# A selective-scan megakernel: the silus of x and z in four half-sized instructions a segment, and the last dt block's pieces at other steps

## What is computed

```python
def _mamba(x, in_w, conv_w, conv_b, xproj_w, dt_w, dt_b, A_log, D, out_w):
    xz = einsum('bld,ed->ble', x, in_w); xi, z = split(xz, 2)
    xi = silu(_dw_conv(xi, conv_w, conv_b))           # 512 channels, 4 taps
    dtr, Bm, Cm = split(einsum('bld,ed->ble', xi, xproj_w))
    dt = softplus(einsum('blr,dr->bld', dtr, dt_w) + dt_b)
    for t:  h = exp(dt_t * A) * h + (dt_t * x_t) * B_t ;  y_t = sum_s h * C_t     # 16 states per channel
    y = (y + xi * D) * silu(z)
    return einsum('bld,ed->ble', y, out_w)
fwd = _mamba(h, fm...) ; bwd = _mamba(flip(h), bm...)
```

## Time and profile before

| | us |
|---|---|
| median of 3 runs | 1098.32 |
| lowest, highest | 1097.88, 1099.91 |
| profiled execution, its own time | 1099.44 |
| its span | 1097.7 |

### The profile page before, as it was taken

How to read it: one execution, slowest core, us unless ns; L and a number is a source line. 1 busy time by engine, 2 the same in 40 slices (tenths; PEclk the granted TensorE clock), 3 DMA queues, 4 the chain that set the end, 5 groups by cost and what they waited for, 6 DMA issues and landing times. The chain is left out here.

```text
span 1097.7 us, 13218 instructions
## 1 busy us (share of the span) xinstructions
PE 959.0 (87%) x3836; PEld 600.4 (55%) x3836; DVE 873.2 (80%) x1136; ACT 560.8 (51%) x1204; POOL 703.3 (64%) x505
## 2 busy tenths in 40 slices
PE   5898867999999999995969977989889987787798
PEld 2566646888888888883424422433444342332487
DVE  3788677777778778776579899988998999999853
ACT  2687632333333333322667766766577467564141
POOL 3377623555555555541289799989998899999000
PEclk9899988999999999997979999989999899999999
DMA  3000025442442442313065555654545455664001
GB/s 102 1 2 0 1 110 152 123 134 82 119 134 88 112 134 94 108 39 91 13 161 155 163 152 145 147 161 142 153 140 157 125 146 154 153 154 115 0 1 39
DMA packets 60033, 115.32 MB, mean 105 GB/s; under 512 B 10400, under 2 KB 15776, under 8 KB 59856
## 3 DMA queue, kind: packets, MB, share of 16 engines
q1 hardware_dynamic: 58848, 112.87, 36.7%
q10 hardware_dynamic: 1136, 1.90, 0.5%
HBM read 113.24 MB, written 1.51 MB: 105 GB/s over the span
## 5 line engine op out<-in xcount | busy, mean ns | idle before, releaser
L1649 POOL TENSOR_TENSOR uB<-u,rows_B 128x512 f32<-128x512 f32 x256 | 320.4, 1282 | 17.1 <-DVE da L1799 13.7
L870 POOL TENSOR_TENSOR lutw<-lutw,lt 128x865 f32<-128x865 f32 x80 | 184.9, 2312 | 164.9 <-DVE lt L836 159.1
L1818 PE MATMUL ya<-hV,ident 128*128 128x512 f32 x336 | 189.6, 651 | 62.6 <-DVE hV L1741 61.9
L1799 DVE TENSOR_TENSOR_SCAN da<-da,uB 128x512 f32<-128x512 f32 x168 | 201.0, 1220 | 17.2 <-ACT da L1728 12.3
L1818 PEld LDWEIGHTS ya<-hV,ident 128*128 128x128 f32 x336 | 61.3, 201 | 158.9 <-DVE hV L1741 123.4
L1658 POOL TENSOR_TENSOR hP<-hS,rows_C 128x512 f32<-128x512 f32 x88 | 112.7, 1281 | 21.8 <-issue 8.5
L1727 ACT ACTIVATE da<-zero 128x2 f32<-128x2 f32 x256 | 43.0, 168 | 152.0 <-DVE hV L1741 151.7
L1796 DVE TENSOR_TENSOR_SCAN hS<-da,uB 128x512 f32<-128x512 f32 x88 | 106.7, 1212 | 16.0 <-ACT da L1727 7.5
L1741 DVE TENSOR_TENSOR hV<-da,rows_C 128x512 f32<-128x512 f32 x168 | 112.6, 671 | 0.0
L744 ACT ACTIVATE ah<-ups 128x1024 fp32r<-128x1024 f32 x40 | 41.2, 1029 | 130.0 <-DVE ups L832 130.0
L829 DVE TENSOR_TENSOR si<-gps,cwb 128x1024 f32<-128x1024 f32 x40 | 49.0, 1225 | 57.1 <-ACT gps L741 53.4
(11 more groups left out here) (341 smaller groups left out, 2034.8 us busy)
## 6 DMA issues: line engine op xcount, KB each, us to landing
rows_B<-bc_rows SPq DMA_DIRECT2D x128, 256.0 KB, 3.6
rows_C<-bc_rows SPq DMA_DIRECT2D x128, 256.0 KB, 4.3
wr<-in_moe_w SPq DMA_DIRECT2D x40, 384.0 KB, 4.8
cwb<-cw_rows SPq DMA_DIRECT2D x16, 512.0 KB, 4.0
cwb<-cw_rows SPq DMA_DIRECT2D x16, 384.0 KB, 5.0
cwb<-cw_rows SPq DMA_DIRECT2D x16, 256.0 KB, 4.1
lut_f<-in_lut_idx SPq DMA_DIRECT2D x1, 2160.0 KB, 10.3
cwb<-cw_rows SPq DMA_DIRECT2D x16, 128.0 KB, 4.4
```

The source lines that it names most:

```text
L870: e.tensor_tensor(part, part, lt[:, q, :], ALU.add).then_inc(s_la, 1)
L1649: e.tensor_tensor(uB[:, n % UBUF, :], u[:, seg % 2, d, :], RB[:, q, :], ALU.mult).then_inc(s_ub, 1)
L1799: e.tensor_tensor_scan(a[:, way], a[:, way], uB[:, n % UBUF, way], 0.0, ALU.mult, ALU.add).then_inc(s_sc, 1)
L1818: return e.matmul(ya[n % 2][:, :], g.ident[:, :], at, start=False, stop=False, skip_group_check=True).then_inc(done, 1)
```

## The change

`silu_x` and `silu_z` each take a half h and work on two blocks (128x1024 instead of 128x2048), with their own table load behind. For the next segment, x's halves stand at steps 23 and 31 (before: all at 31); z's halves stand at step 62 of the segment before and at step 4 (before: all at 4). The matmul of dt block 3 moves from step 15 to step 12, its `parts` from 22 to 18, `exp` from 24 to 20, `log` from 25 to 22, its softplus on DVE from 25 to 22, and `keep_dt` from 29 to 27. In the last segment the first four of them move from 15, 21, 22, 23 to 12, 18, 20, 22.

```diff
@@ project_tensor, rows_tensor
-                              (11, x_tensor(e, k, 2)), (13, conv_tensor(e, k, 1)), (15, None), (16, x_tensor(e, k, 3)),
+                              (11, x_tensor(e, k, 2)), (12, None), (13, conv_tensor(e, k, 1)), (16, x_tensor(e, k, 3)),
-            e.wait_ge(s_xi, DB + k)
+            e.wait_ge(s_xi, DB + 2 * k)
@@ scalar
-        def silu_x(e, k):
-            e.wait_ge(s_cv, DB * k)
-            e.activation(xi[:, k % 2, :, :], xi[:, k % 2, :, :], ACT.Silu).then_inc(s_xi, 1)
-        def silu_z(e, k):
-            e.wait_ge(s_zc, DB * (k + 1))
-            e.activation(sz[:, k % 2, :, :], sz[:, k % 2, :, :], ACT.Silu).then_inc(s_sz, 1)
+        def silu_x(e, k, h):
+            two = slice(2 * h, 2 * h + 2)
+            e.wait_ge(s_cv, DB * (k - 1) + 2 * h + 2)
+            e.activation(xi[:, k % 2, two, :], xi[:, k % 2, two, :], ACT.Silu).then_inc(s_xi, 1)
+            e.preload_act_table_set("natural_log_exp_and_others")
+        def silu_z(e, k, h):
+            two = slice(2 * h, 2 * h + 2)
+            e.wait_ge(s_zc, DB * k + 2 * h + 2)
+            e.activation(sz[:, k % 2, two, :], sz[:, k % 2, two, :], ACT.Silu).then_inc(s_sz, 1)
+            e.preload_act_table_set("natural_log_exp_and_others")
@@ project_scalar
             yield 18
             copy_x(e, k, 2)
+            parts(e, k - 1, 3)
+            yield 20
+            exp(e, k - 1, 3)
             yield 21
             copy_conv(e, k, 1)
             newest_tap(e, k, 2)
             yield 22
-            parts(e, k - 1, 3)
+            log(e, k - 1, 3)
             yield 23
             copy_x(e, k, 3)
-            yield 24
-            exp(e, k - 1, 3)
-            yield 25
-            log(e, k - 1, 3)
+            silu_x(e, k, 0)
             yield 26
             copy_conv(e, k, 2)
             newest_tap(e, k, 3)
-            yield 29
+            yield 27
             keep_dt(e, k - 1, 3)
             yield 30
             copy_conv(e, k, 3)
             yield 31
-            silu_input(e, k)
+            silu_x(e, k, 1)
@@ first_scalar, middle_scalar (the end of each)
+            yield 62
+            silu_z(e, k, 0)
@@ begin_scalar
             yield 4
-            silu_z(e, seg)
-            e.preload_act_table_set("natural_log_exp_and_others")
+            silu_z(e, seg, 1)
@@ side_vector
-            yield 25 if k < NSEG else 23
+            yield 22
             softplus(e, seg, 3)
```

More of the change, by code:

```diff
@@ L1251, in side_tensor @@
             if k == NSEG:
-                yield 15
+                yield 12
                 dt_tensor(e, seg, 3)
@@ L1362, in keep_dt @@
             e.activation(dt[:, k % 2, d, :], DTB[d][:, :], ACT.Copy).then_inc(s_dtc, 1)
-        def silu_input(e, k):
-            silu_x(e, k)
-            e.preload_act_table_set("natural_log_exp_and_others")
         def first_dt_scalar(e):
@@ L1466, in first_scalar @@
             split_scalar(e, 3)
+            yield 62
+            silu_z(e, 1, 0)
         def begin_scalar(e, seg):
@@ L1518, in middle_scalar @@
             copy_z(e, k, 1)
+            yield 62
+            silu_z(e, k, 0)
         def last_scalar(e):
             yield from begin_scalar(e, NSEG - 1)
-            yield 21
+            yield 18
             parts(e, NSEG - 1, 3)
+            yield 20
+            exp(e, NSEG - 1, 3)
             yield 22
-            exp(e, NSEG - 1, 3)
-            yield 23
             log(e, NSEG - 1, 3)
@@ L1747, in gate @@
                     e.wait_ge(s_ap, pool_steps(last))
-                    e.wait_ge(s_sz, seg) if seg else e.wait_ge(s_zc, DB)
+                    e.wait_ge(s_sz, 2 * seg) if seg else e.wait_ge(s_zc, DB)
                     e.tensor_tensor(sz[:, seg % 2, d, :], ya[b][:, :], sz[:, seg % 2, d, :], ALU.mult).then_inc(s_g, 1)
```

## The result

The changed kernel takes 1104.83 us (median of 5 runs, 1102.23 to 1106.57) against 1098.32 (1097.88 to 1099.91) before. The ratio is 1.0057, with a 95% interval of 1.0043 to 1.0072: it is slower by 6.5 us. The forecast was 1098.0 with a range of 1093.5 to 1104, so it missed, and on the wrong side of "no change". The profiled execution took 1104.0, 4.6 more than the one before (1099.44), so the profile shows most of the loss.

What follows compares the result with a forecast made beforehand. No engine bounds alone; DVE and POOL share the bound, held together by three `uB` buffers. Terms z +4.1, x at 31 -2.55, x at 23 +1.3, PE's clock -4.1 gave -1.2 us: forecast 1098.0, range 1093.5 to 1104.

Steps and rivals of the forecast that it cites:

- I take it that the clock then holds: Behind x's silu near step 32, PE's clock was to stay at full speed; with shorter waits, -4.1 us.
- the part on the PE behind it: PE, some 2.6 us behind after step 24, would reach add 31 with work in hand; 2.03 us idle time gone.
- The wait that it was to shorten, at scan 41: DVE's "issue" wait, 6.5 us over three segments, would shrink to 0.6 to 0.8 each: -4.1 us.
- two gaps of 1.3 us near step 24: PE idle 1.3 us ahead of add 23 and 1.3 ahead of the convolution; no cost in the sum.
- PE's clock still falls: Rival, chance 0.29: clock falls at step 32, sum +2.9; at 24 or 63 up to 1 us a place; 1101 to 1104.
- x's first half: New silu block at step 23 delays scan 24, mostly covered by the moved softplus: +0.45 a segment, +1.3 us for three.
- z: Halves at steps 62 and 4: late scan 63 +6.7, shorter wait at scan 5 -2.55, together +4.1 us.
- x's second half: Still at step 31, shorter block cuts DVE's wait at scan 32 from 2.80 to 1.95: -0.85 a segment, -2.55 us.
- The dt matmul: Dt block 3's matmul, three steps earlier on PE, costs nothing; if it waited for `keep_dt`, some 0.6 us.
- POOL hides the new stalls: Rival, chance 0.23, faster: POOL works on through late scans 63 and 24, most of +6.7 falls away; 1090 to 1095.
- The loads count in full: Rival, chance 0.06, slower: every added silu block adds its fixed cost to the path, +16.7 us: 1116.

Runs made afterwards that it cites:

- Run 5: Changed kernel plus three extra matmuls a segment on PE near step 22, outputs the same; 1098.88 us, ratio 0.9999 to the kernel before.
- Run 8: Kernel before with only x's silu in halves at steps 23 and 31, dt pieces at old steps, z whole; 1100.74 us, ratio 1.0018.
- Run 3: Kernel before with only the pieces of dt block 3 moved, both silus whole at steps 31 and 4; 1093.01 us, ratio 0.9944.
- Run 1: Kernel before with only z's silu split, halves at steps 62 and 4; 1102.6 us, ratio 1.0027.
- run 4: Kernel before with only z's silu split, halves at steps 4 and 36 behind the gates, x as before; 1094.77 us, ratio 0.9967.
- run 2: Changed kernel with z's silu whole again at step 4 (x's halves and dt pieces stay); 1098.33 us, ratio 1.0003 to the kernel before.
- run 10: The changed kernel timed again, nothing altered, on another chip; 1103.8 us, ratio 1.0046 to the kernel before.
- 6: Kernel before with dt pieces moved and z's halves at steps 4 and 36, x whole at 31; 1089.92 us, ratio 0.9919.
- 11: Changed kernel with z's halves at steps 4 and 36 and three extra PE matmuls a segment near step 22; 1093.48 us, ratio 0.995.
- 7: Kernel before with dt pieces moved and x's silu whole at step 36, what follows it four steps later; 1096.42 us, ratio 0.9982.

## Why the prediction was wrong

**The step that failed** is the one that says "I take it that the clock then holds", in the part on the PE behind it. It holds at step 32, and there the term was near, -3.2 against -4.1, but partly by luck. The wait that it was to shorten, at scan 41, is still 1.5 us in each segment at full clock, where I had put 0.6 to 0.8, and gives only 2.0; the other 1.1 comes at scans 34 and 35 of the first segment, which I had not counted. But the prediction itself had worked out two gaps of 1.3 us near step 24, and priced them at nothing in the sum. The gaps were 2.14 + 1.08 and twice 1.40 + 1.08, and the clock fell behind two of the three. That term, put at 0, measured 3.5 us at scan 31. The rival "PE's clock still falls" had the mechanism, yet at a wrong place and price: it looked for the fall at step 32 first, and gave a fall at 24 "up to 1 us a place". Measured were 2.33 and 1.21. Run 5 shows this by filling the gaps and changing nothing else: 5 to 6 us. Run 8 sets a limit to it: a fall at the same place cost nothing where DVE still had its softplus to do behind it. So what the prediction lacked is the fall and the missing slack together.

**The cover was counted to the wrong account.** The prediction let the moved softplus pay for x's first half, +0.45 a segment net, which the trace bears out (0.6). Run 3 shows what that hid: the moved pieces, with no silu beside them, are worth 6.2 us. So the right way to read the change was as a good one (the dt pieces, -6.2), a bad one laid over it (x's halves, +6.5, of which some 2.6 to 3.4 for the block and 3.8 for the clock), and a second bad one (z's halves at 62 and 4). As a sum it comes to the same; as a judgement of the parts it does not.

**z** was right: +7.2 against +6.7 and -2.6 against -2.55, by the mechanism as told. Run 1 confirms it alone and run 4 against it: behind the gates half a block costs 0.3 us, at the segment's end 2.4. On top of run 2, z's halves cost more by the timings, 4.7 to 5.9 us (run 10 and the first timing), than alone, 3.0. Run 2's profile had the slow 3.63 us subtraction in the last segment, the changed kernel's the fast one (last section); with that set right the two traces are 4.9 apart from the first scan to the last, and 4.5 of it is z's own two terms. Alone they are as large in the trace (run 1, 4.1 from the first scan to the last); why the timings of run 1 give only 3.0 is open.

**x's second half** was right (-2.3 against -2.55), and the step from 4.63 to 3.78 us for a block as well (from this load to the exp behind it, 598.56): ACT in the first segment,

```profile
594.78 1.28 ACT L1326 ACT_TABLE_LOAD   x1
596.08 1.06 ACT L1326 ACTIVATE xi<-xi 128x1024 f32<-128x1024 f32 x1
597.15 1.28 ACT L1327 ACT_TABLE_LOAD   x1
```

The dt matmul did not make PE wait, as told. "POOL hides the new stalls" is refuted: scan 63's lateness is kept in full up to scan 2 of the next segment. "The loads count in full" is refuted by run 4. The rule of the Trainium skill, "ScalarE: Activation LUTs", "Table sets: the hidden batching unit", to do all work of one table set before switching, agrees with the outcome for x, where the whole silu is faster in runs 3 and 6, and not with z, where two halves at good places gain 0.85 and lose 0.35.

**What stays open.** Why the clock holds in the second segment and falls in the third, with the same two gaps. In run 2 it is the other way round, and in run 10, the changed kernel again, as in its first trace. The Trainium skill, "TensorE: Matmul & The Clock Gate", Part 1, says that the chip's watch over activity runs free of the program, and so varies from run to run. The rows are in keeping with it, 1.40 + 1.08 us at clock 1.00 and 1.39 + 1.08 at 0.53, but no run here sets it apart from other causes. Open too is why the gain behind scan 32 in the third segment is 0.6 us both where the clock falls there (run 3, 848.2 to 851.6) and where it does not (the changed kernel).

## What to carry to other kernels

When a change moves a stall, follow the idle time of the engine with a variable clock too: here two gaps of 1 to 2 us close together on PE cost 3.5 us in scans that stand seven steps later, on another engine. Ask as well what slack stands behind the fall: where a softplus kept DVE busy for 1.3 us, as short a fall cost nothing (run 8). A block that stops an in-order pipeline costs what the others cannot fill at that place, so look for the place (behind the gates 0.3 us, at the segment's end 2.4) before making it smaller or more frequent. And cost the pieces of a bundled change one by one: the part that looked like mere preparation was worth 6 us, and the parts it prepared for lost over 12.

## What was not expected of the hardware

The first of the table's subtractions in the last segment, on DVE with all operands in SBUF, takes either of two times. Before, on DVE and on POOL at the same moment:

```profile
1003.25 3.64 DVE L1552 TENSOR_TENSOR lut_l<-lutw,lut_h 128x540 fp32r<-128x540 f32 x1
```

```profile
1002.57 3.73 POOL L1649 TENSOR_TENSOR uB<-u,rows_B 128x512 f32<-128x512 f32 x3
```

and after:

```profile
1008.52 1.21 DVE L1556 TENSOR_TENSOR lut_l<-lutw,lut_h 128x540 fp32r<-128x540 f32 x1
```

```profile
1007.88 4.19 POOL L1653 TENSOR_TENSOR uB<-u,rows_B 128x512 f32<-128x512 f32 x3
```

In the one, DVE's instruction ends at 1006.89, 0.59 behind POOL's run of three, which runs at its own speed (3.73); in the other DVE is through in 1.21, and POOL takes 4.19. It may be that the two share a way into SBUF and the one that has it keeps it; that is a guess, and no run here tried it by itself. The Trainium skill, "GPSIMD Engine Reference", section "1. Specifications", lists the SBUF interfaces as shared with VectorE, with contention for DVE instructions with two SBUF inputs among others; the rows agree. This is the -2.43 us at scan 57 in the table's row for the last segment. The profile of run 10, the same program as the changed kernel, has 3.64 at that place, so the swing is one of executions and no property of the edits. It was 3.63 to 3.64 in the traces of runs 1 to 5 and 8 to 11 as well, and 1.20 in those of 6 and 7.

And matmuls that compute nothing can pay for themselves: three more a segment, some 0.9 us each at full clock, gave back 5 to 6 us in the changed kernel.
